# Graph layers on one core: score terms in row strips, values as weights in column strips, and a longer pipeline of slots

## What is computed

```python
h = relu(layernorm(x))                               # per graph, x is [128, 128]
hw = (h @ W).reshape(128, 4, 32)                     # values of 4 heads
e = (hw * a1).sum(-1)[:, None] + (hw * a2).sum(-1)[None]   # per head, [node, node]
e = leaky_relu(e, 0.2); e = where(adj > 0, e, -9e15)
x = x + softmax(e, -1) @ hw                          # layer 0
h = relu(layernorm(x)); x = x + relu((h + adj @ h) @ W1 + b1) @ W2 + b2    # layer 1 (eps = 0)
h = relu(layernorm(x)); x = x + adj @ (h @ W3) + b3                        # layer 2
h = relu(layernorm(x)); x = x + gru5(h, adj) * mask                        # layer 3
```

## Time and profile before

| | us |
|---|---|
| three runs | 678.94, 679.14, 677.99 |
| median | 678.94 |
| profiled execution | 678.75 |
| its span | 676.6 |
| busy in the span: TensorE, VectorE, ScalarE, GpSimd | 650.1, 590.2, 528.1, 408.3 |
| granted TensorE clock, mean | 0.995 of full |

### The profile page before, as it was taken

The page is one execution under the profiler, slowest core; times in us unless marked ns, Lnnn a source line. Parts: engine busy times, 40 slices in busy tenths (PEclk is TensorE's granted clock), DMA queues, the critical chain, the costliest instruction groups (busy, mean ns, idle before and its releaser), DMA issues. The chain is left out here.

```text
span 676.6 us, 13204 instructions
## 1 busy us (share of the span) xinstructions
PE 650.1 (96%) x4380; PEld 425.2 (63%) x4380; DVE 590.2 (87%) x1349; ACT 528.1 (78%) x964; POOL 408.3 (60%) x367
## 2 busy tenths in 40 slices
PE   5899999999999999999999999999999999999995
PEld 3678888888888888875555445555555555455552
DVE  3777787777788777798999899999999999999995
ACT  3688888888888888876787787877878777878774
POOL 4556676676666666564666655555555555555554
PEclk9999999999999999999999999999999999999997
DMA  6111111110011110003332233333343333333432
GB/s 161 32 33 32 32 32 32 32 32 26 10 31 33 32 32 17 1 17 62 49 57 54 47 63 63 79 79 73 68 63 78 78 79 68 58 79 79 78 76 65
DMA packets 114690, 35.82 MB, mean 53 GB/s; under 512 B 87680, under 2 KB 114624, under 8 KB 114624
## 3 DMA queue, kind: packets, MB, share of 16 engines
q1 hardware_dynamic: 113424, 34.79, 24.1%
q10 hardware_dynamic: 1200, 0.20, 0.2%
HBM read 9.80 MB, written 4.19 MB: 21 GB/s over the span
## 5 line engine op out<-in xcount | busy, mean ns | idle before, releaser
L1561 POOL TENSOR_TENSOR h0T<-r,zh 128x512 f32<-128x512 f32 x80 | 103.3, 1291 | 141.8 <-DVE r L1598 138.9
L52 PE MATMUL psum<-h_parts,gru_w 128*128 128x512 f16 x720 | 182.1, 379 | 2.7 <-DVE r L1602 1.8
L52 PE MATMUL psum<-t_parts,gru_w 128*128 128x512 f16 x720 | 181.5, 379 | 1.4 <-DVE t_parts L1585 1.4
L52 PEld LDWEIGHTS psum<-h_parts,gru_w 128*128 128x128 f16 x720 | 69.0, 98 | 85.2 <-DVE r L1602 16.5
L52 PEld LDWEIGHTS psum<-t_parts,gru_w 128*128 128x128 f16 x720 | 66.6, 98 | 68.2 <-DVE t_parts L1585 11.1
L1555 POOL TENSOR_TENSOR zh<-z,h0T 128x512 f32<-128x512 f32 x80 | 103.0, 1288 | 8.6 <-ACT z L1533 8.6
L1530 ACT CAST t_parts<-psum 128x512 f16<-128x512 f32 x80 | 46.9, 586 | 59.7 <-PE psum L52 59.6
L691 POOL TENSOR_TENSOR prob<-prob,row_max 128x512 f32<-128x512 f32 x64 | 68.8, 1088 | 22.2 <-DVE row_max L1179 20.4
L1443 DVE CAST h_parts<-h0T 128x512 f16<-128x512 f32 x80 | 80.3, 1004 | 1.9 <-POOL h0T L1561 1.9
L1538 ACT ACTIVATE r<-r,gates_b 128x512 f32<-128x512 f32 x80 | 65.0, 813 | 10.2 <-DVE r L1589 6.5
L1533 ACT ACTIVATE z<-psum,gates_b 128x512 f32<-128x512 f32 x80 | 62.3, 779 | 5.7 <-PE psum L52 0.9
(11 more groups left out here) (135 smaller groups left out, 1199.1 us busy)
## 6 DMA issues: line engine op xcount, KB each, us to landing
x_all<-in_x SPq DMA_DIRECT2D x16, 256.0 KB, 3.4
adj<-in_adj SPq DMA_DIRECT2D x16, 256.0 KB, 3.0
out_x<-y SPq DMA_DIRECT2D x14, 256.0 KB, 2.5
h_nodes<-h_parts SPq DMA_TRANSPOSE x80, 3.1
out_x<-zT SPq DMA_DIRECT2D x2, 256.0 KB, 2.3
gw<-in_L_gnn_weight SPq DMA_DIRECT2D x1, 320.0 KB, 6.1
W<-in_L_gnn_W SPq DMA_DIRECT2D x2, 128.0 KB, 2.8
wi<-in_L_gnn_w_ih SPq DMA_DIRECT2D x1, 192.0 KB, 6.9
```

The source lines that it names most:

```text
L52: return nc.tensor.matmul(out, lhsT, rhs, start=start, stop=stop)
L1561: pool.tensor_tensor(state(now), by_graph(r[now.s][:, :]), by_graph(zh[now.s][:, :]), ALU.add)\
```

## The change

Attention:
- `score_w` shrinks to 32 columns. Four matmuls, one per graph, write to 32 partitions each of B_EDGE (columns 0 to 127), so the terms of four graphs lie in four strips of rows. `e_parts` becomes 128x128: `keep_e` casts to `e_high`, and `keep_e_lo` makes both parts at once with a column `lo_rows` that is -1 on the rows of the low part and 0 elsewhere.
- Masks become units of their own. `scores` runs over all four graphs: four `pick_i` matmuls, each contracting over 32 rows and each into its graph's bank, then `pick_j` with the four graphs inside each head.
- `attend` takes the values of a head as weights (128x32) and the probabilities as moving operand (128 columns); the four heads write to four strips of 32 partitions of bank 0. The result is turned. The column of ones goes; `sum_up` adds 16 matmuls with `sum_ones` (128x32) as weights into four strips of bank 1.
- DVE copies both results to SBUF (`attT` 128x512, `sumT` 128x128), TensorE turns them back (five transposes) into banks 3 and 2, and `divide` works there.
- `pick_i` and `pick_j` are made by two ScalarE copies from a small table that three VectorE reductions and a multiplication make (`sum_rows`), not on GpSimd.

Order: 19 slots in place of 17. `at(0)` is centred, `at(1)` scaled and turned, `at(2)` has scores, exponentials and transposes, `at(3)` attention, `at(4)` layer 1, `at(5)` layer 2, `at(6)` the last normalisation, `at(7)` its turn. GpSimd's `normalise` is split into `centre` and `scale`. Loads of x run one pair of groups further ahead than those of adj. `remaining` gets one group's last normalisation and two last turns more, and one `root` (a power on GpSimd) for another group.

```diff
         def score_terms(group):
-            mm(nc, P[:, B_EDGE, :], t["score_w"][:, :], hT[:, :]).then_inc(e_psum, 1)
+            for g in range(GROUP):
+                last = mm(nc, P[g * ROWS:(g + 1) * ROWS, B_EDGE, 0:NODES], t["score_w"][:, :],
+                          hT[:, g * 128:(g + 1) * 128])
+            last.then_inc(e_psum, 1)
...
+        def mask(group, g):
+
+            if g == 0:
+                pe.wait_ge(gone_ready, group.count)
+            wait_users(pe, ([att_kept, sums_kept, rsum_done, x_attended][g], group.before(1)))
+            mm(nc, P[:, g, :].rearrange("p (h m) -> p h m", h=HEADS), t["identb"][:, :],
+               gone[group.odd][:, g, :].unsqueeze(1).to_broadcast([128, HEADS, NODES]), True, False)
+
+        def scores(group):
+
             pe.wait_ge(e_lo, group.count)
...
+            for g in range(GROUP):
+                rows = slice(g * ROWS, (g + 1) * ROWS)
+                mm(nc, P[:, g, :].rearrange("p (h m) -> p h m", h=HEADS), e_parts[group.odd][rows, :],
+                   t["pick_i"][rows, :, :], False, False)
             for h in range(HEADS):
-                last = mm(nc, bank[:, h, :], t["pick_j"][:, h, :], e, False, h == HEADS - 1)
-            last.then_inc(score_ready, 1)
+                for g in range(GROUP):
+                    rows = slice(g * ROWS, (g + 1) * ROWS)
+                    last = mm(nc, P[:, g, h * 128:(h + 1) * 128], t["pick_j"][rows, h, :],
+                              e_parts[group.odd][rows, :], False, h == HEADS - 1)
+                    if h == HEADS - 1:
+                        last.then_inc(score_ready, 1)
...
+        def attend(group, half):
+
+            pe.wait_ge(probT_act, group.half_count(2 * half))
+            pe.wait_ge(probT_dve, group.half_count(2 * half))
             pe.wait_ge(hW_ready, group.count)
+            for g in range(2 * half, 2 * half + 2):
+                for h in range(HEADS):
+                    dims = slice(h * HEAD_DIM, (h + 1) * HEAD_DIM)
+                    last = mm(nc, P[dims, 0, g * 128:(g + 1) * 128], hW[group.odd][:, g, dims], probT[:, g, h, :])
+            if half == 1:
+                last.then_inc(att_psum, 1)
+
+        def sum_up(group):
+
             for h in range(HEADS):
-                last = mm(nc, P[:, g, h * (HEAD_DIM + 1):(h + 1) * (HEAD_DIM + 1)], probT[:, g, h, :],
-                          hW[group.odd][:, g, h, :])
-            if g == GROUP - 1:
-                last.then_inc(att_psum, 1)
+                for g in range(GROUP):
+                    last = mm(nc, P[g * ROWS:(g + 1) * ROWS, 1, 0:NODES], t["sum_ones"][:, h * ROWS:(h + 1) * ROWS],
+                              probT[:, g, h, :], h == 0, h == HEADS - 1)
+            last.then_inc(sums_psum, 1)
+
+        def turn_attended(group):
+            pe.wait_ge(att_kept, group.count)
+            turn(3, attT).then_inc(back_psum, 1)
+
+        def turn_sums(group):
+            pe.wait_ge(sums_kept, group.count)
+            nc.tensor.transpose(P[:, 2, 0:128], sumT[:, :], t["ident"][:, :]).then_inc(sums_back, 1)
...
+            v.scalar_tensor_tensor(e_parts[group.odd][:, :], e_high[:, :], t["lo_rows"][:, 0:1],
+                                   P[:, B_EDGE, 0:NODES], ALU.mult, ALU.add).then_inc(e_lo, 1)
...
-        for p in range(GROUPS // 2):
-            for q in range(2):
-                one_slot(p, q, p * 2 + q)
-        one_slot(GROUPS // 2, 0, GROUPS)
+        for number in range(LAST + 4):
+            one_slot(number // 2, number % 2, number)
```

More of the change, by code:

```diff
@@ new lines, in slot @@
+            if number == 3:
+                gru.fuse(pe, 3)
+            if number == 2:
+                pe.wait_ge(score_weights.picks, 2)
+                pe.wait_ge(score_weights.eyes, 4)
+                pe.wait_ge(gru.kept, 2)
+            if at(2):
+                mask(at(2), 0)
+                mask(at(2), 1)
+            if at(4):
+                hidden(at(4), 0, B_TURN,
+                       (h0T_kept, at(4).before(3)), (hT_ready, at(4).before(-2)), (x_added[0], at(4).before(1)), (hid_ready[0], at(4).before(1)))
+                hidden(at(4), 1, B_SUM)
@@ new lines, in slot @@
+            if at(2):
+                mask(at(2), 2)
+                mask(at(2), 3)
+                scores(at(2))
+            if at(5):
+                neighbours(at(5), 1, B_EDGE, adjT[at(5).odd], adjT_ready,
+                           (e_lo, at(5).before(-3)), (x_added[1], at(5).before(1)), (z_ready[1], at(5).before(1)))
+            if number == 2:
+                gru.turn(pe, 2)
+            if number == 3:
+                gru.fuse(pe, 4)
+            if at(4):
+                out_0(at(4))
@@ L896, in slot @@
-            if number == 0:
                 gru.turn(pe, 0)
@@ new lines, in slot @@
+            if number == 4:
+                act.wait_ge(gru.layers_loaded, gru.all_layers_loaded)
+            if at(4):
+                normalise(at(4), 1)
+            if at(5):
+                rstd_of(at(5), 2)
+            if at(7):
+                keep_h0T(at(7), B_TURN)
+            if at(2):
+                keep_e(at(2))
+            if number == 2:
+                gru.keep_fused(act, 0)
+            if number == 8:
+                gru.keep(act, 3)
+            if at(6):
+                rstd_of(at(6), 3)
@@ new lines, in slot @@
+            if at(5):
+                keep_z(at(5), 1, B_EDGE)
+            if number == 2:
+                gru.keep(act, 2)
+            if number == 3:
+                gru.keep_fused(act, 4)
+            if at(3):
+                rstd_of(at(3), 1)
+            if number == 2:
+                act.wait_ge(score_weights.made, 1)
+            if at(2):
+                exponential(at(2), 0)
+            if at(3):
+                keep_adjT(at(3))
+            if at(2):
+                exponential(at(2), 1)
+                keep_probT(at(2), 0)
```

630 lines of the change are left out of this document (307 added, 323 removed).

## The result

| | us |
|---|---|
| before, beside it | 679.04 (677.99 to 679.87) |
| after, median | 650.72 (649.03 to 652.16) |
| ratio | 0.9575 (95% interval 0.9557 to 0.9593) |
| profiled execution, span | 651.48, 649.3 |
| forecast | 663 (648 to 688), A alone 648 to 676 |

The kernel is 28 us faster, the sign is the forecast's and the time lies in A's range, but 12 us under its centre. Four readings of the changed kernel show where that comes from.

A forecast was written before the change was run, and what follows sets the result against it. TensorE's stream was taken to set the unit, falling from 18.03 to 16.69 us. Steps between groups -22.7, tail +5.3 and recurrent part +1.4 gave -16.0 from 678.75: 663 us, range 648 to 688.

The forecast's parts named there:

- A: TensorE's strips run side by side at 0.028 to 0.047 us a pass: 648 to 676, centre 663; chance 0.55.
- D: Strips on TensorE do not overlap at all, 0.111 us a pass, picks as now: about 750 us; chance 0.08.
- B: On TensorE, two passes of one fp32 matmul block the strip order, 0.055 us a pass: centre 683 us; chance 0.24.
- dear changes of mode: Switching TensorE between whole array and strips costs 0.17 us a change, 0.28 us more a unit than taken.
- four changes of mode: TensorE switches between whole array and strips four times a unit, at 0.10 us each: 0.40 us (0 to 0.68).
- what does not change (the rest of the unit): TensorE's other matmuls in a unit, outside the 6.93 of 18.03 us that change, carried over at their old price: 11.10 us.
- the pace, 0.040 a pass: How often TensorE starts a pass when neighbours use different strips: 0.040 us, between 0.028 and 0.055; 72 passes cost 2.88.
- The floor of 15.7: VectorE and ScalarE, each busy 14.9 us a unit and keeping some waits between dependent steps, allow no unit under about 15.7.
- The fill: Early units hold less work, so the 15 steps between groups take 5 us under the steady pace: 245.4 us.
- Tail: From group 15's scores to the first recurrent matmul: 20.7 us instead of 15.4, 5.3 later.
- Start and recurrent part: Start of group 0's scores unchanged (0 to +2 us); recurrent part 0.9 longer for two transposes, 0.5 for other engines' work.
- C: The new order leaves TensorE waiting about 0.9 us a unit on a ring of copies, division and masks: 676 us; chance 0.13.

The follow-up runs named there:

- same_strip_in_a_row: The changed kernel with attention and sums reordered so that all passes of one strip come in a row, then the next strip: 671.22 us, ratio 0.9872.
- score_strips_alone_at_once: The kernel before, in its old order, with only the score part in strips and all four masks and the scores ahead of out_1: 689.00 us, ratio 1.0129.
- masks_wait_for_x: The changed kernel with each mask waiting until the group before is added to x, not until its own bank is read: 680.58 us, ratio 1.0011.

## Why the prediction was right, and where it was off

**Sign and mechanism: right.** Strips run side by side (A), and the parts in strips gave most of a unit's gain: the changed parts went from 6.93 to 4.47 us (the first five rows of the table below), 2.46 of 3.35. D is out (0.91 us of attention, not 3.5). B is out as it was put: two passes of one strip in a row do not block the next strip, since a strip takes four. Its second part, dear changes of mode, is out as well: 0.10 each, as taken. By the Trainium skill, TensorEngine Tiling (Array Packing), section Tiling Modes, Key Properties, a change drains the engine; the trace shows 0.10 and not the 0.17 that I had as the price of a full emptying. The other rule of the Trainium skill that the prediction names, in TensorE: Matmul & The Clock Gate, Part 3, that matmuls start in program order, does not hold between strips here: in the sums of same_strip_in_a_row the second strip starts before three passes that precede it in the program.

**The unit: 14.68, not 16.69.** By the terms of the sum (predicted, measured):

| term | predicted | measured |
|---|---|---|
| 72 passes in strips | 2.88 | 2.11 (0.91 + 0.99 + 0.21) |
| five transposes | 0.59 | 0.55 |
| masks | 0.86 | 0.86 |
| pick_i, pick_j | 0.22 + 0.64 | 0.23 + 0.32 |
| four changes of mode | 0.40 | 0.40 |
| what does not change (the rest of the unit) | 11.10 | 10.21 |
| unit | 16.69 | 14.68 |

The step that failed first is the pace, 0.040 a pass: it was chosen between two bounds by the row of a matmul whose stream sets the pace, and the measured 0.029 (2.11 / 72) is all but the lower bound, 0.028. `pick_j` at 0.020 lies even lower, with four strips of fp16. The second failure is that the unchanged matmuls were carried over at their old price. They held 0.9 us of slack, of which the busy share of 17.83 in 18.03 showed 0.2:

```profile
121.00 1.16 PE L52 MATMUL psum<-adjT,y 128*128 128x128 f32 x8
122.34 0.38 PE L52 MATMUL psum<-gone,identb 128*128 128x512 bf16 x1 [0.19 <-DVE x_all L1199]
```

In the kernel before, these eight passes cost 1.34 from start to start, and the same eight elsewhere 0.89; in the new order both cost 0.89 beside the change of mode. So the next mask comes 0.45 us late in each unit, and the row names for what: VectorE's addition to x. The wait column gives 0.19 of it, since the last pass is still recorded as running in the rest. This is how the prediction came to read 1.9 us of waits in 220 as no waits. With the 16 transposes of prob and `out_0` some 0.7 of the 0.9 is found. The forecast compared groups of one unit with each other only for the parts that change.

**The floor of 15.7: wrong.** VectorE was put at 14.9 and has 13.09, ScalarE at 14.9 and has 14.55, and "keep some waits between dependent steps" did not hold for ScalarE, which is busy 99%. For VectorE about 1.0 of the 1.8 us is seen: `shift` takes 0.6 less a unit, and the cast `edges` 416 ns instead of 774. Both ran beside GpSimd in the kernel before: `shift` ended with GpSimd's addition, and `edges` started at 147.62 during a subtraction that ended at 148.10, and ended 0.28 after it; in the changed kernel nothing runs beside it in four units of five. That moving them would have shortened the kernel before was not run. The floor also made A's low end: 648 was given for a unit of 15.7, and the unit came out under it. (The 15.6 given there for TensorE with free mode changes is a slip too: 11.10 + 2.02 + 0.59 + 0.86 + 0.22 + 0.45 is 15.24.)

**The fill: wrong in sign.** Taken at 5 us under the steady pace, it was 8.7 over it (228.9 against 15 x 14.68 = 220.2), 13.7 us of the gain given back. The prediction counted what early slots have less, while their length is that of one group's softmax, which was named in the same sentence and not priced; as the steady pace fell, it stood out more. It had no term for the granted clock either, which falls to 0.79 in three stretches of the start; how much of the 13.7 that is stays open. **Tail:** 23.4, not 20.7; waits were taken at 2 us, and one of 1.58 (above) and one of 0.67 for attT are seen. The rest was not followed up. **Start and recurrent part:** 1.2 and 2.7 instead of 0 and 1.4; the latter has a wait of 2.31 for a last y at 273.56.

Summed up against the forecast of -16.0: unit 15 x -2.01 = -30.2, fill +13.7, tail +2.7, start +1.2, recurrent part +1.3, so -27.3. Errors of opposite sign, -30.2 and +18.9, brought the time to within 12 us of the forecast. That the time lies in the stated range is luck in this sense: with the unit alone put right the sum gives 663 - 30.2 = 633, well below 648. The answer that C was unlikely is right for this kernel, but its reason ("most of a unit to be used") is not: with one wait set on the whole group, 2.07 us a unit came back.

## What to carry to other kernels

Work with 32 rows or 32 columns costs about a quarter when four strips are fed in turn, fp32 included (0.36 for the small fp16 `pick_j`); keep at most four passes of one strip in a row and few changes between strips and the whole array. Before trusting a saving on a full engine, build the order that lets the others keep up: here the score strips in the old order made the kernel slower than before, and the whole change with one coarse wait was worth nothing. When a unit is costed, compare each unchanged group with its cheapest occurrence in the trace, and look for small instructions with long durations: here they were waits that no wait column shows.

## What the runs showed of the chip

- An fp32 pass of 128 columns costs 0.029 us when four column strips are fed in turn, against 0.111 for the whole array. A strip takes four passes, the running one included; a fifth holds back all that follows (2.37 us against 0.99 for the same 32 passes, 1.04 with four in a row).
- A change between strips and whole array costs 0.10 us here (0.09 to 0.11 at the four places of a unit).
- A VectorE instruction of 128x4 that starts 0.10 us after a GpSimd addition of 128x512 takes 1.20 us instead of 0.15 to 0.25, and everything behind it on VectorE waits. By the Trainium skill, Advanced Engine Details and Errata, GPSIMD Details, the two share a read and write interface; the rows agree.
- With the score part alone, a wait of about 2.1 us for y in a unit goes with a granted clock of 0.91 to 0.93 in most stretches, where the kernel before has 1.00. With a wait of 1.16 (score_strips_alone_at_once) most units have 1.00; three are some 1.4 us longer, and the one of these in a window has 0.91. But masks_wait_for_x has a wait of 1.90 in each unit and 1.00 from 80 to 240 us; from 240 to 250 it has 0.83, and that unit takes 18.44 us and not 16.75. Why the one and not the other stays open.
